# Layer 3's softmax with unscaled weights, one exponential a step, and mean squares packed four units at a time

## The reference, cut to what matters

```python
qkv = silu(x @ w_qkv.T)
q, k, v = jnp.split(qkv, 3, axis=-1)
q_flat = apply_rope(rms_norm(q.reshape(B, L, H, D), w_qn))
k_flat = apply_rope(rms_norm(k.reshape(B, L, H, D), w_kn))
...
scores = jnp.einsum('blhd,blwhd->blhw', q_flat, k_win) * scale
soft_mask = sigmoid((width - rel_dist) * sharp)
scores = scores - (1.0 - soft_mask) * 10000.0
attn = softmax(scores, axis=-1)
out = jnp.einsum('blhw,blwhd->blhd', attn, v_win).reshape(B, Hs, Ws, C)
out = rms_norm(out, w_on)
return silu((out + v) @ w_out.T)
```

## Time and profile before

| | us |
|---|---|
| three runs | 3361.9, 3371.34, 3377.48 |
| median | 3371.34 |
| the profiled execution | 3381.97 |
| its span, first to last instruction | 3380.1 |
| layer 3 in the span, from about | 2588 to 3380 |

### The profile page before, as it was taken

One profiled execution on the slowest core, in us unless ns is written; L12 is line 12 of the kernel. 1 busy time (PEld: TensorE's weight loads), 2 busy tenths in 40 slices (PEclk: granted clock), 3 DMA queues, 4 the chain that ended last, 5 costly groups with the idle time before them and its releaser, 6 DMA issues. The chain is left out here.

```text
span 3380.1 us, 103119 instructions
## 1 busy us (share of the span) xinstructions
PE 3018.3 (89%) x43264; PEld 1668.5 (49%) x43264; DVE 2138.1 (63%) x5157; ACT 1995.5 (59%) x4348; POOL 1134.3 (34%) x1444
## 2 busy tenths in 40 slices
PE   6999999999985899999999977999995788888886
PEld 2333333333322565555565645667663555555553
DVE  5787778878753676767667643554553466665654
ACT  2667676766662556455556533555552677777774
POOL 3443433434311221222222201222221455554643
PEclk9999999999986999999999988999996899999997
DMA  6877778687763233333333214545444233333332
GB/s 200 163 170 153 172 171 179 143 187 162 145 142 114 62 86 81 73 89 86 86 69 81 67 47 148 159 150 169 149 148 145 69 92 115 117 115 113 117 103 76
DMA packets 299756, 414.89 MB, mean 123 GB/s; under 512 B 39424, under 2 KB 256288, under 8 KB 278304
## 3 DMA queue, kind: packets, MB, share of 16 engines
q1 hardware_dynamic: 275664, 272.46, 27.1%
q0 software_dynamic: 18432, 134.23, 19.9%
q10 hardware_dynamic: 5200, 1.62, 0.2%
HBM read 219.67 MB, written 53.81 MB: 81 GB/s over the span
## 5 line engine op out<-in xcount | busy, mean ns | idle before, releaser
L734 DVE TENSOR_TENSOR l_probs<-l_psum,l_decay 128x1024 f32<-128x1024 f32 x512 | 598.6, 1219 | 164.7 <-PE l_psum L630 154.0
L782 ACT ACTIVATE l_sizes<-l_probs 128x2048 f32<-128x2048 f32 x256 | 487.1, 1908 | 303.2 <-DVE l_probs L734 292.1
L1822 ACT ACTIVATE l_logits<-l_logits,l_low 128x100 f32<-128x100 f32 x1024 | 372.7, 366 | 203.4 <-DVE l_low L1802 202.7
L1829 POOL TENSOR_TENSOR l_logits<-l_logits,l_inv 128x400 f32<-128x400 f32 x256 | 242.9, 950 | 679.9 <-DVE l_inv L1808 679.2
L630 PE MATMUL l_psum<-l_qk 32*128 32x512 f32 x2048 | 340.2, 645 | 7.9 <-POOL l_qk L868 4.2
L883 POOL DMA_DIRECT2D l_sizes<-l_sizes x128 | 111.5, 871 | 549.3 <-ACT l_sizes L782 537.3
L1645 POOL TENSOR_TENSOR l_E<-l_E,l_causal 128x1024 f32<-128x1024 f32 x64 | 153.0, 2390 | 381.6 <-DVE l_x_act L1343 224.6
L645 PE MATMUL l_psum<-l_probs,l_V 128*32 128x512 f32 x2048 | 270.6, 600 | 1.7 <-DVE l_probs L734 1.6
L1814 DVE COPY l_PT<-l_psum 100x512 f32<-100x512 f32 x256 | 173.0, 676 | 114.4 <-PE l_psum L1774 113.9
L301 PE MATMUL l_psum<-l_xT,l_w_up 128*128 128x512 f32 x512 | 231.3, 606 | 9.1 <-DVE l_row_var L1401 9.0
L1789 PE MATMUL l_psum<-l_PT,l_V_windows 100*32 100x16 f32 x16384 | 202.6, 187 | 34.9 <-issue 22.6
(11 more groups left out here) (246 smaller groups left out, 5883.8 us busy)
## 6 DMA issues: line engine op xcount, KB each, us to landing
l_sizes<-l_sizes POOLq DMA_DIRECT2D x128, 1024.0 KB, 7.6
l_V_windows<-v_image SPq DMA_DIRECT2D x512, 100.0 KB
l_V_windows<-v_padded SPq DMA_DIRECT2D x512, 100.0 KB
l_E<-rows_c SPq DMA_DIRECT2D x64, 512.0 KB, 5.8
l_xT<-y SPq DMA_DIRECT2D x24, 1024.0 KB, 5.3
y<-l_res SPq DMA_DIRECT2D x32, 512.0 KB, 3.1
l_e_everywhere<-rows_e SPq DMA_DIRECT2D x112, 128.0 KB, 5.6
l_xT<-x SPq DMA_DIRECT2D x8, 1024.0 KB, 11.3
```

The costliest lines, as they stand in the source:

```text
L734: nc.vector.tensor_tensor(probs[:, N % 2, 2 * p:2 * p + 2, :], ring.region(name).rearrange("p (a n) -> p a n", a=2), decay[:, h:h + 2, s0: ...
L782: nc.scalar.activation(sizes[:, slot(N), :, :], probs[:, N % 2, :, :], ACT.Abs).then_inc(sized, 1)
L1822: nc.scalar.activation(e, e, ACT.Exp, scale=-1.0, bias=self.low[:, N % 4, i:i + 1], accum_out=self.total[:, N % 4, i:i + 1]).then_inc(self ...
L1829: nc.gpsimd.tensor_tensor(p, p, self.inv[:, N % 4, :].unsqueeze(2).to_broadcast([P, STEP, NKEY]), ALU.mult).then_inc(self.p_ready, 1)
```

## The change

In layer 3 alone, `SummedTiles` replaces `Tiles`.

- The weights stay unscaled. GpSimd's `lower` subtracts `low` from a step's 400 columns, and one exponential of 128 x 400 without a bias or a sum follows on ScalarE. `invert` and `scale` are gone.
- `weigh` puts two steps into one PSUM bank, two banks in turn: columns 0 to 255 hold the outputs of the two channel halves, columns 256 to 511 the sums of the weights, which eight more matmuls a step make against a 100 x 32 tile of ones, so that each channel of a head gets its head's sum.
- VectorE's `divide(R)` takes the reciprocal of a bank's 256 sum columns and multiplies the 256 output columns into `OT`, at odd steps, for steps N - 5 and N - 4. `copy_out` is gone; `out_squares` squares `OT` in steps 3 and 11. `out_mean` goes from steps 3 and 11 to steps 4 and 12, ahead of that step's units, `finish` of the first half from step 12 to step 13, behind the queries' scaling.
- Four units share a mean: `head_mean` is 128 x 32, a head's mean lies in eight rows, and four matmuls into four row blocks of one ring slot make a pack. `root_of_mean` runs once for a pack (2 an image instead of 8). `spread` takes it back to 128 channels, with a 32 x 128 matrix per unit on that unit's 32 rows, two units and two ring slots at a time. VectorE multiplies from the ring slot. Packs lie in steps 12 and 14, spreads in 13, 14, 15 and in step 3 of the next image. Before the scores of step 0 TensorE waits until six units are scaled, before those of step 8 for the last two.
- `square` gets four buffers instead of three, `rec` two instead of four, `OT` two instead of one; one small constant more is loaded.

```diff
+        if N % 2 == 0 and R >= 2:
+            pe.wait_ge(self.o_copied, R - 1)
+        c0 = self.bank(R)
...
+        for g in range(HALVES):
+            for a in range(4):
+                p = self.place(N, 4 * g + a)
+                out = self.ps[a * HD:(a + 1) * HD, c0 + (2 + g) * P:c0 + (3 + g) * P].rearrange("p (r t c) -> p t r c", r=TILE, c=TILE)
+                of = self.pt[0:NKEY, N % 2, :].rearrange("p (i h r c) -> p i h r c", i=STEP, h=NH, c=TILE)
+                m = nc.tensor.matmul(out[:, N % 2 * STEP:(N % 2 + 1) * STEP], self.ones[0:NKEY, :], of[:, :, p],
+                                     start=True, stop=True)
+        m.then_inc(self.weighed, 1)
...
+    def exps(self, nc, act, N):
+        act.wait_ge(self.lowered, N + 1)
+        p = self.logits[:, N % 4, :, :]
+        nc.scalar.activation(p, p, ACT.Exp, scale=-1.0).then_inc(self.p_ready, 1)
+    def lower(self, nc, pool, N):
+        pool.wait_ge(self.l_ready, STEP * (N + 1))
+        p = self.logits[:, N % 4, :, :]
+        nc.gpsimd.tensor_tensor(p, p, self.low[:, N % 4, :].unsqueeze(2).to_broadcast([P, STEP, NKEY]),
+                                ALU.subtract).then_inc(self.lowered, 1)
...
 MEANS = (("q", 0, 0), ("q", 0, 1), ("k", 0), ("k", 1), ("k", 2), ("k", 3), ("q", 1, 0), ("q", 1, 1))
-MEANS_AT = {12: (0, 2), 13: (2, 4), 14: (4, 6), 15: (6, 8)}
-ROOTS_AT = {12: (0, 2), 13: (2, 4), 14: (4, 6), 15: (6, 7)}
-SQUARES_AT = {10: (0, 2), 11: (2, 3), 12: (3, 4), 13: (4, 6), 14: (6, 8)}
-KEYS_AT = {14: (0, 1), 15: (1, 4)}
+PACK = 4
+PACK_AT = {12: 0, 14: 1}
+SQUARES_AT = {10: (0, 2), 11: (2, 4), 12: (4, 6), 13: (6, 8)}
+SPREAD_AT = {13: (0, 2), 14: (2, 4), 15: (4, 6)}
+LAST_SPREAD = 3
...
+                def mean(b, m):
+                    name = ("mean", b, m)
+                    pe.wait_ge(sq_ready, 8 * b + PACK * (m + 1))
                     ring.may_fill(pe, name)
-                    nc.tensor.matmul(ring.region(name), head_mean[:, :], square[:, j % 3, :], start=True,
-                                     stop=True).then_inc(ring.filled(name), 1)
+                    for u in range(PACK):
+                        i = nc.tensor.matmul(ring.region(name)[32 * u:32 * u + 32, :], head_mean[:, :], square[:, u, :], start=True,
+                                             stop=True)
+                    i.then_inc(ring.filled(name), 1)
+                def spread(b, j0):
+                    pe.wait_ge(r_ready, 2 * b + j0 // PACK + 1)
+                    for j in (j0, j0 + 1):
+                        ring.may_fill(pe, ("rec", b, j))
+                    for j in (j0, j0 + 1):
+                        r = slice(32 * (j % PACK), 32 * (j % PACK) + 32)
+                        nc.tensor.matmul(ring.region(("rec", b, j)), head_spread[r, :], rec[r, j // PACK, :], start=True,
+                                         stop=True).then_inc(ring.filled(("rec", b, j)), 1)
...
                         w.turn(nc, pe, N - 2)
                     if 3 <= N < B * STEPS + 3:
                         w.weigh(nc, pe, N - 3)
+                    if n == 4 and b > 0:
+                        out_mean(b - 1, 1)
+                    if n == 12 and b < B:
+                        out_mean(b, 0)
                     for u in layer3_units(n):
                         if unit_name(u, b) is not None:
                             unit(unit_name(u, b))
                     if b + 1 < B:
-                        for j in range(*MEANS_AT.get(n, (0, 0))):
-                            mean(b + 1, j)
-                    if n == 3 and b > 0:
-                        out_mean(b - 1, 1)
-                    if n == 11 and b < B:
-                        out_mean(b, 0)
+                        for j in range(*SPREAD_AT.get(n, (0, 0)), 2):
+                            spread(b + 1, j)
+                        if n in PACK_AT:
+                            mean(b + 1, PACK_AT[n])
+                    if n == LAST_SPREAD and 0 < b < B:
+                        spread(b, 6)
...
-                    dve.wait_ge(r_ready, 8 * b + u + 3)
+                    name = ("rec", b, u + 2)
+                    ring.is_full(dve, name)
...
+                def divide(R):
+                    c0 = w.bank(R)
+                    s = slice(R % 8 * P, (R % 8 + 1) * P)
+                    dve.wait_ge(w.weighed, 2 * (R + 1))
+                    if R >= 2:
+                        dve.wait_ge(w.o_copied, R - 1)
+                    vstep(dve, nc.vector.reciprocal(w.share[:, R % 2, :], PS[:, c0 + 2 * P:c0 + 4 * P]))
+                    nc.vector.tensor_tensor(OT[R // 8 % 2][:, :, s], PS[:, c0:c0 + 2 * P].rearrange("p (g t) -> p g t", g=HALVES),
+                                            w.share[:, R % 2, :].rearrange("p (g t) -> p g t", g=HALVES), ALU.mult).then_inc(w.o_copied, 1)
...
-                    if 1 <= N < B * STEPS + 1:
-                        w.invert(nc, dve, N - 1)
                     if 2 <= N < B * STEPS + 2:
                         w.copy_turned(nc, dve, N - 2)
+                    if n % 2 == 1 and 4 < N < B * STEPS + 5:
+                        divide(N // 2 - 2)
...
                     if b + 1 < B:
-                        if n in (13, 14):
-                            scale_query(b + 1, n - 13)
-                        for u in range(*KEYS_AT.get(n, (0, 0))):
-                            scale_key(b + 1, u)
-                    if n in (3, 4) and 0 < b < B:
-                        scale_query(b, 3 + n)
+                        for j in range(*SPREAD_AT.get(n, (0, 0))):
+                            if MEANS[j][0] == "k":
+                                scale_key(b + 1, number_of(j))
+                            else:
+                                scale_query(b + 1, j)
+                    if n == LAST_SPREAD and 0 < b < B:
+                        scale_query(b, 6)
+                        scale_query(b, 7)
                     if n in (5, 7) and b > 0:
                         finish(b - 1, 1, n // 2 - 2)
-                    if n == 12 and b < B:
+                    if n == 13 and b < B:
                         finish(b, 0, 0)
                         finish(b, 0, 1)
...
+                    if b > 0:
+                        ring.is_full(act, ("rec", b - 1, PACK * m + 3))
+                    nc.scalar.activation(rec[:, m, :], ring.region(name), ACT.Ln, bias=eps4[:, :]).then_inc(ring.took(name), 1)
                     ring.is_taken(act, name)
-                    nc.scalar.activation(rec[:, j % 4, :], rec[:, j % 4, :], ACT.Exp, scale=-0.5).then_inc(r_ready, 1)
+                    nc.scalar.activation(rec[:, m, :], rec[:, m, :], ACT.Exp, scale=-0.5).then_inc(r_ready, 1)
...
-                    if n == 10 and b < B:
-                        copy_out(b, 0)
+                    if n == 11 and b < B:
+                        out_squares(b, 0)
...
-                    if n == 11 and b < B:
+                    if n == 12 and b < B:
                         nc.scalar.preload_act_table_set("natural_log_exp_and_others")
                         root_of_out(b, 0)
                     if b + 1 < B:
+                        if n in PACK_AT:
+                            root_of_mean(b + 1, PACK_AT[n])
...
-                for N in range(B * STEPS + 1):
+                for N in range(B * STEPS):
                     b, n = step_of(N)
-                    if N > 0:
-                        w.scale(nc, pool, N - 1)
+                    w.lower(nc, pool, N)
```

153 lines of the change are left out of this document (83 added, 70 removed).

## The result

The changed kernel takes 3461.09 us (median of four runs, 3432.41 to 3468.36), the kernel before 3374.41 (four runs, 3361.9 to 3384.88): a ratio of 1.0243 with a 95% interval of 1.0174 to 1.0311. It is slower, as forecast, but by 87 us and not by 27, and it lies outside the forecast's range. The profiled execution took 3462.76 us, its span is 3461.0 (before: 3380.1).

What follows compares the result with a forecast made beforehand. ScalarE was taken to bound scores 12 to scores 0, TensorE the projections. Boundaries +27, scores 0 to 4 -4, scores 4 to 12 +1, start +2, end +1 make +27 us on 3371.34: 3398, range 3368 to 3438.

Steps and rivals of the forecast that it cites:

- the chain over four engines: Scores 12 to scores 0: replaces ScalarE as bound, VectorE's queue order its longest piece; 23.8 us instead of 19.86.
- the clock's price: Scores 0 to 4, behind the boundary: TensorE's lower granted clock, +10 at the upper end if four more images fall.
- the forecast's +27: Boundary, scores 12 to scores 0: 23.8 us in place of 19.86, +3.9 an image, +27 us in seven.
- the row of four elements: Profile row for VectorE's reciprocal: 172 ns at four elements, a copy 160; basis for 1.2 to 1.9 us at 256.
- D: VectorE's new work every second step, reciprocal and product of 128x256: 1.85 us taken, bounds 0.85 and 2.1.
- Runs the chain once without finish, 0 to 4: Layer 3's start, before the first scores: one pass of the chain, +2 us, between 0 and 4.
- Scores 0 to 4 and 4 to 12: The two stages after the boundary: -0.6 and +0.2 us an image, -4 and +1 in seven.
- D is covered there: Scores 4 to 12: odd steps divide while TensorE fills two projections; without that cover 3 x 1.85 us.
- Faster: Rival: links overlap, TensorE idles no more at the boundary than today's 3.8 us; 18.5 us there, 3343 in all; chance 0.15.
- no change: Rival: VectorE's reciprocal runs at a copy's pace, +8 us, 3379; chance 0.25.
- Division dearer: Rival: VectorE's reciprocal and product take 2.4 us, the boundary 24.9; +39 in all, 3410; chance 0.10.
- In turn: Rival: TensorE's packs and spreads run serially, a pack 4.3 us; +60 over the forecast, 3458; chance 0.05.

Runs made afterwards that it cites:

- the filled kernel: The changed kernel with 18 unread identity products on TensorE before each second pack and 9 at the end of step 15: 3443.64 us, ratio 1.0187.
- the softmax alone: The kernel before with only the softmax part (sums, division, one exponential, moved output means and finish), eight means as before: 3448.79 us, ratio 1.0187.
- the queue cleared: The changed kernel with divisions in even steps, finish behind step 15's keys and the second pack before the second spread: 3429.56 us, ratio 1.0160.
- cleared and filled: The changed kernel with even-step divisions, finish behind the keys, second pack first, and 6 identity products at steps 14 and 15 each: 3423.84 us.
- all moves: The changed kernel with finish and a division behind the last keys, other divisions in even steps, earlier second packs, 8 and 5 identity products: 3426.94 us.

## Why the prediction was right in its sign and wrong in its size

**The mechanism held.** ScalarE ceased to bound the boundary, and the chain over four engines took its place, with the second pack behind the first key and scores 0 behind the last. Counted from scores 12, the boundary shown above ends its queries at 13.3 us (forecast 12.6), finish at 16.1 (15.4), gives the first key at 18.8 (18.2), the last at 26.1 (23.8). Up to the second pack the steps are right to 0.7 us.

**The step that failed most is the clock's price.** It stood in the forecast as +10 in all, at the upper end alone, for four images that fall, and inside the boundary at nothing. All seven boundaries fell, and not only the stage behind them. The forecast had the two waits on TensorE, 4.5 us and one for the keys, and yet priced the pack behind them at full speed, 1.06. It was 1.94. Filled waits give 1.9 us a boundary back, some 15 in seven with what the sixth gives beside its stall. That is half of the 31 us by which the boundaries went beyond the forecast's +27; the stall of the sixth is 4 and the divisions are 5, and some 7 stay open.

**The division.** The reciprocal is 1745 ns, at the upper side of the 1.2 to 1.9 us that the row of four elements gave; D is 2.20, from the start of the reciprocal at 2943.65 to the end of the product, instead of 1.85, just past the forecast's bound of 2.1. From 172 ns at four elements to 1745 at 256 it is 6.2 ns an element, where that row's two readings gave 4.0 and 7 and I went between. The Trainium skill's "VectorE: DVE Perf Modes", section "First, the fixed hardware budget", with a repeat count of 8, gave an estimate of 2.1 us; the measured value lies midway between that and mine. Two divisions on the chain, the first and the last, make 0.7 of the 1.4 us by which the filled boundary exceeds 23.8.

**The start.** "Runs the chain once without finish, 0 to 4" was wrong: +8.3. From the first mean to the first scores, the windows of before and of after:

```profile
2643.72:2657.64 13.92, 10.78 (x16) 3.13 (x16) 5.84 (x8) 11.88 (x21) 0.00 (x0) 0.83 0.43 127
```

```profile
2652.57:2672.97 20.40, 12.10 (x32) 2.50 (x32) 5.54 (x8) 4.75 (x8) 0.00 (x0) 0.50 0.32 96
```

TensorE has nothing else to do there. Eight means in a row kept TensorE at .83; two packs and four spreads, each waiting for another engine, ran at 0.50, the lower of the clock's two levels, from end to end, a pack in 1.94 us and a spread pair in 2.08:

```profile
2660.94 2.08 PE L2460 MATMUL l_psum<-l_rec,l_head_spread 32*128 32x512 f32 x4 [2.90 <-DVE l_q_blocks L2620]
2663.91 1.94 PE L2450 MATMUL l_psum<-l_square,l_head_mean 128*32 128x512 f32 x8 [0.89 <-DVE l_keys L2590]
2667.31 2.08 PE L2460 MATMUL l_psum<-l_rec,l_head_spread 32*128 32x512 f32 x4 [1.46 <-ACT l_rec L2746]
```

The other 1.8 us lie ahead of the first pack, which by the program waits for four squares where the first mean waited for one.

**Scores 0 to 4 and 4 to 12.** Forecast -0.6 and +0.2 an image, measured +0.5 and +0.9, the second no more than the spread of its images. I had counted the division in the first only as a delay of the group average; without sums and reciprocal that stage is 2.0 us shorter. In the second, taking out either the sums or the reciprocal gives 0.6 to 0.9: whether "D is covered there" was too much is not told from the spread.

**What was right in size.** A pack 1.06 us, a spread pair 1.13 (1.0 taken), the exponential, the product; the sums too. In the chain of work of the filled kernel they stand behind the weigh matmuls with 0.28 us, beside 0.25 forecast (their busy time of 0.50 a step overlaps the weigh's):

```profile
2947.13 0.63 PE l_psum L1870 x48
2947.77 0.28 PE l_psum L1878 x16
```

**The rivals.** Faster and no change are out. "Division dearer" had the direction, but D is 2.20 and not 2.4, and the time is 51 us above its 3410. "In turn" gave 3458, near the time by luck: its mechanism isn't there, as a pack takes 1.06 us and not 4.3.

## What to carry to other kernels

Where a change replaces many independent matmuls by a few that wait for other engines, price the matmuls behind a long wait at the slower clock too (here the pack behind 4.36 us took 1.94 us, while the spread behind 0.95 us took its full-speed 1.13), and ask for the clock that the same stretch has when it already waits. Behind an engine that is busy for all of a stage, the next chain may be as long: here ScalarE's 6.5 us at the boundary were worth nothing in the time even when sums and reciprocal were left out. And an operation of which only a tiny row exists is worth its dear end in the sum, not a value between.

## What the runs showed of the hardware beside this

- A reciprocal of 128x256 out of PSUM takes 1745 ns, four times the product of the same width (425 ns).
- TensorE stands for 0.2 to 4.4 us with nothing in the profile to wait for, on average 2.4 us an image before, 3.9 after and 6.8 with the softmax alone (idle spans of its timeline marked as issue, images 1 to 6, without those before the scores of step 0, which end with VectorE's last key). Of a boundary such spans are 1.9 us after and 0.2 before; how much of that lies on the path was not shown. In the changed kernel one of 4.10 us lies in the sixth boundary and makes it 32.2 us; the output mean behind it ran at the lower clock:

```profile
3237.47 0.65 PE L1878 MATMUL l_psum<-l_PT,l_ones 100*32 100x64 f32 x15 [4.10 <-issue]
3238.05 3.32 PE L2478 MATMUL l_psum<-l_O_square,l_all_mean 128*128 128x512 f32 x4
```

  The same step of the same image has 4.39 us with the queue cleared, 3.16 cleared and filled and 2.34 with all moves; in the kernel with 27 products in the waits, where more instructions stand ahead of it, the longest in that boundary is 1.38. The instruction queue moved 344 packets before and 361 after (5.64 and 5.91 MB). The Trainium skill, "Runtime: NRT & Kernel Launch", section "Instruction fetch mechanics", says that TensorE's instructions are brought in blocks by a queue of the engine's own, mostly hidden. That these stalls are such a fetch was not shown.
- Layers 0 to 2 and the first norm behind them, the same in all kernels, ended anywhere within 31 us (2594 to 2625). Where one layer is changed, its own length in the trace says more than the span.
